# One block of values and sums per unit, and two heads' softmax sums by PE, in an attention and expert kernel

## The reference

```python
xn = layernorm(x)
q = (xn @ Wq.T).reshape(b, t, 8, 32)
kv = xn @ Wkv_down.T                     # rank 64
k = (kv @ Wk_up.T).reshape(b, t, 8, 32)
v = (kv @ Wv_up.T).reshape(b, t, 8, 32)
attn = softmax(einsum('bqhd,bkhd->bhqk', q, k) * 32 ** -0.5)
a = einsum('bhqk,bkhd->bqhd', attn, v).reshape(b, t, 256) @ Wo.T
e = mod(floor(xn @ wr + br), 8)          # the expert of each token
y = relu(xn @ W1[e] + b1[e]) @ W2[e] + b2[e]
out = x + a + y
```

## Time and profile before

| what | before |
|---|---|
| median of 3 runs | 508.03 us (506.31 to 508.95) |
| the profiled execution | 507.6 us |
| its span, first to last instruction | 505.8 us |
| mean granted clock of TensorE | 0.97 |
| busy: PE / DVE / Pool / ACT | 90% / 83% / 77% / 69% |
| first stage, units 2 to 15 | about 86 to 231 us of the span |
| second stage, units 16 to 31 | about 344 to 504 us of the span |

### The profile page before, as it was taken

How to read it: one execution, slowest core, us unless ns; L and a number is a source line. 1 busy time by engine, 2 the same in 40 slices (tenths; PEclk the granted TensorE clock), 3 DMA queues, 4 the chain that set the end, 5 groups by cost and what they waited for, 6 DMA issues and landing times.

```text
span 505.8 us, 15098 instructions
## 1 busy us (share of the span) xinstructions
PE 453.2 (90%) x4992; PEld 318.6 (63%) x4992; DVE 418.0 (83%) x885; ACT 347.1 (69%) x864; POOL 388.0 (77%) x407
## 2 busy tenths in 40 slices
PE   1577886999899898998999999998999999999997
PEld 1356443656566464656999999994657656666565
DVE  6998964768998999977888788886698898988986
ACT  3777463767777677766777777774577667876775
POOL 5546287888888988883777777776788888989883
PEclk9985797999999999999999999999899999999999
DMA  8794233444757678589687888845356565765522
GB/s 233 227 181 128 63 79 84 107 96 95 204 123 186 164 224 235 153 260 252 211 264 245 271 262 280 257 152 116 83 124 134 142 128 118 149 134 128 111 80 89
DMA packets 81930, 83.07 MB, mean 164 GB/s; under 512 B 10608, under 2 KB 66384, under 8 KB 81872
## 3 DMA queue, kind: packets, MB, share of 16 engines
q1 hardware_dynamic: 77520, 73.40, 54.5%
q0 software_dynamic: 4352, 8.92, 7.7%
HBM read 38.61 MB, written 18.37 MB: 113 GB/s over the span
## 4 chain that ended last, share of the span: by engine, by line
PE 43%; POOL 24%; DVE 9%; issue 9%; DMA 8%; ACT 4%; SPq 3%; ACTq 0%; POOLq 0%; DVEq 0%
POOL xsort L602 11%; POOL padd L633 11%; PE psum L1286 5%; PE psum L1409 5%; PE psum L1270 4%; PE psum L1251 4%; DMA stk<-mT 4%; PE psum L1392 3%; PE psum L1410 3%; PE psum L1393 3%; PE psum L1394 3%; DVE negm L992 3%; PE psum L1328 3%; SPq L328 2%; PE psum L1301 2%
## 5 line engine op out<-in xcount | busy, mean ns | idle before, releaser
L719 ACT ACTIVATE prob<-psum 128x512 f32<-128x512 f32 x256 | 150.1, 593 | 101.7 <-PE psum L1270 100.9
L992 DVE TENSOR_REDUCE negm<-psum 128x2 f16<-128x512 f32 x256 | 170.3, 681 | 42.1 <-PE psum L1251 41.2
L633 POOL TENSOR_TENSOR padd<-prob 128x512 f32<-128x512 f32 x104 | 125.7, 1209 | 27.7 <-ACT prob L719 21.3
L1251 PE MATMUL psum<-stk 96*128 96x256 f16 x512 | 101.2, 280 | 12.9 <-DVE negm L992 11.6
L584 POOL TENSOR_TENSOR padd<-xTl,padd 128x512 f16<-128x512 f32 x71 | 82.3, 1159 | 32.6 <-DVE padd L1104 32.6
L1270 PE MATMUL psum<-stk 97*128 97x256 f16 x512 | 97.5, 274 | 5.9 <-DMA stk<-mT 3.8
L789 ACT ACTIVATE xTl<-psum,xn_all 128x128 f32<-128x128 f32 x284 | 81.1, 369 | 26.7 <-POOL padd L584 18.1
L602 POOL DMA_INDIRECT xsort<-xn_all,pos x64 | 71.7, 1121 | 15.7 <-issue 13.7
L1251 PEld LDWEIGHTS psum<-stk 96*128 96x128 f16 x512 | 42.2, 98 | 54.1 <-DVE negm L992 28.3
L610 POOL DMA_INDIRECT xn_all<-ysort,pos x64 | 66.0, 1031 | 11.1 <-issue 7.9
L1286 PE MATMUL psum<-prob,vt 128*32 128x256 f32 x1024 | 70.2, 393 | 0.0
(11 more groups left out here) (171 smaller groups left out, 890.9 us busy)
## 6 DMA issues: line engine op xcount, KB each, us to landing
stk<-split SPq DMA_DIRECT2D x192, 128.0 KB
xn_all<-wsplit SPq DMA_DIRECT2D x71, 258.0 KB, 4.7
xTh<-xsort SPq DMA_DIRECT2D x18, 256.0 KB, 4.2
ysort<-xTh SPq DMA_DIRECT2D x18, 256.0 KB, 4.6
out<-acc SPq DMA_DIRECT2D x15, 256.0 KB
acc<-x SPq DMA_DIRECT2D x3, 1024.0 KB, 8.4
xn_all<-W SPq DMA_DIRECT2D x12, 256.0 KB
wsplit<-xn_all SPq DMA_DIRECT2D x12, 256.0 KB, 3.3
```

The costliest lines, as they stand in the source:

```text
L633: nc.gpsimd.tensor_tensor(padd[:, bb, hs], prob[:, bb, hs, 0, :], prob[:, bb, hs, 1, :], ALU.add).then_inc(pool_add, 1)
L719: nc.scalar.activation(prob[:, bb, h, :, :].rearrange("p a c -> p (a c)"), bank[st_bank(u, n)], ACT.Exp, scale=SCALE).then_inc(act_exp, 1)
L992: V.tensor_reduce(negm[:, k % 2, col:col + 2], bank[n % 2].rearrange("p (a c) -> p a c", a=2), AX.X, ALU.max, negate=True).then_inc(dve_ma ...
L1251: ins = mm(bank[n % 2][:, qc * T:(qc + 1) * T], stk[0:96, s, 1, h, t0 + qc * P:t0 + (qc + 1) * P], stk[0:96, s, 0, h, t0:t0 + T], start=Tr ...
```

## The change

Three edits. Pool no longer adds the key chunks behind pair 3 (heads 2 and 3 of the first batch); it adds behind pairs 1 and 5, and in the second stage also 6. PE instead sums these two heads from the two chunks, with four matmuls that accumulate in place of two. And the two places of values and sums on PE become one: both batches' blocks stand at n = 4, behind the scores of pair 4 and the v projection, the second batch of unit u-1 first and the first batch of unit u behind it. In the last two units the sums are those of before, at the new place.

```diff
@@ Pool
-                    if u < NU - 2 and n in (1, 3, 5, 6)[:3 + u // (NU // 2)]:
+                    if u < NU - 2 and n in ((1, 5, 6) if u >= NU // 2 else (1, 5)):
@@ sums
-                    pe.wait_ge(pool_add, u * 4 - NU // 2 + 2 * bb + 2 if half else u * 3 + bb + 2)
+                    pe.wait_ge(pool_add, u * 3 - NU // 2 + 2 * bb + 1 if half else u * 2 + bb + 1)
                     if bb == 1:
                         pe.wait_ge(dve_add, u + 1)
-                for h in range(HG):
+                whole = 2 if bb == 0 and not late else HG
+                for h in range(whole):
                     ins = mm(bank[4 + bb][h * HD:(h + 1) * HD, T:2 * T], ones[:, 0:HD], padd[:, bb, h, :],
                              start=True, stop=True)
+                for kc in range(2):
+                    for h in range(whole, HG):
+                        ins = mm(bank[4 + bb][h * HD:(h + 1) * HD, T:2 * T], ones[:, 0:HD], prob[:, bb, h, kc, :],
+                                 start=(kc == 0), stop=(kc == 1))
                 ins.then_inc(pe_pv, 1)
@@ body of PE
-                        if n == 2 and not f:
-                            values(u * 2 - 1, k + 3, 1, it * 2 + (k + 1) // 2 * 2)
-                            sums(u - 1, 1, last and k == 3, half)
...
-                        if n == 7:
+                        if n == 4:
+                            if not f:
+                                values(u * 2 - 1, k + 3, 1, it * 2 + (k + 1) // 2 * 2)
+                                sums(u - 1, 1, last and k == 3, half)
                             values(u * 2, k, 0, sbu * 2 + 1, u + 2 if nxt else u + 1)
                             sums(u, 0, last and k >= 2, half)
```

## The result

The kernel after takes 571.98 us (median of 4 runs, 569.67 to 574.16) against 508.49 for the kernel before beside it (506.31 to 510.52): a ratio of 1.126, 95% interval 1.120 to 1.131. It is 63.5 us slower; the forecast was 54 us slower, 562, with a range of 545 to 578. The profiled execution took 574.16, the longest of the four, with a span of 572.3 and a mean granted clock of 0.961.

A forecast was written before the change was run, and what follows sets the result against it. Pool was taken to bound the first stage and PE the second. Terms of 26.1 - 2.0 + 4 + 20.0 + 2.4 + 3.6 gave +54 us on 508, so 562, with 0.8 lying within 545 to 578.

The forecast's parts named there:

- PE's leg and the block's length: PE from transpose to scores 5: 1.15 us plus a merged block of 3.30, making 4.45.
- Two legs in series: Each unit: PE's leg of 4.45 us, then DVE's of 5.97 in the second stage, one waiting for the other.
- Odd unit 12.73: Second stage, odd units: output projection behind pair 5 and residual add 1.89 us to 10.84, giving 12.73.
- First stage: Units 4 to 13, before the experts: 127.2 us against 107.2, so +20.0.
- Even unit 11.2: Second stage, even units: 11.0 us with the q projection's wait, 11.2 with the expert sum slowed beside a Pool addition.
- Units 17 to 30: Second stage, transpose 17 to transpose 30: 129.3 us becomes 156.3 less 0.9 for missing projections, +26.1.
- The end: From the last transpose on: exp of pair 4 waits for later sums, output projection uncovered; +4 us (0 to +5).
- Rival 3, the clock: PE's idle waits lower its clock and a quarter of its legs double, +32 us: 594; chance 0.10.
- Up to unit 4: Start to unit 4's transpose: Pool's 1.25 us and a slow block gained, units 2 and 3 lose 3.7; +2.4.
- Pool's relief is swallowed: Less Pool work, worth at most 1.2 us a unit, gains nothing: new legs exceed Pool's old period of 10.98.
- Rival 1: Legs overlap and Pool's relief shows, DVE idling under about 0.5 us a unit behind the block: 503; chance 0.06.
- Rival 2: Transpose's wait or v copy costs less than laid out, about 1 us a unit less over 29 units: 533; chance 0.10.

The follow-up runs named there:

- e1: Kernel before with only Pool's pair 3 addition dropped and PE summing heads 2 and 3, both blocks at their old places: 506.78 us, ratio 0.998.
- e6: Kernel after, but heads 2 and 3 of the first batch take the sums of heads 0 and 1, two matmuls instead of four: 565.49 us, ratio 1.103.
- e3: Kernel after with the second batch's block back behind pair 2, the first batch's staying behind pair 4: 534.37 us, ratio 1.050.
- e4: Kernel after with the first batch's block back behind pair 7, the second batch's staying behind pair 4: 554.32 us, ratio 1.091.
- e7: Kernel after with DVE's addition of the experts' results moved from n = 6 to n = 4: 576.88 us, ratio 1.126.
- e9: Kernel after, but from unit 17 Pool's second-batch additions take only 16 of 256 columns of each head: 573.91 us, ratio 1.120.
- e12: Kernel before, unchanged, run again on a third chip for another trace: 512.58 us.
- e10: Kernel before with only Pool's pair 3 addition given to PE, blocks unmoved, a repeat on another chip: 524.69 us, ratio 1.021.

## Why the prediction was right, and where it was off

The terms, between the same transposes in the two traces:

| stretch | forecast | measured |
|---|---|---|
| up to the transpose of unit 4 | +2.4 | +5.5 (106.69 to 112.15) |
| units 4 to 14 | +20.0 | +20.4 (107.2 to 127.6) |
| unit 14 to 16, through the experts | +3.6 | +4.9 |
| unit 16 to 17 | -2.0 | -2.3 (12.63 to 10.29) |
| units 17 to 30 | +26.1 | +31.0 (129.3 to 160.2) |
| the end | +4 | +7.2 (16.4 to 23.6) |
| sum | +54 | +66.5 |

- *PE's leg and the block's length*: right to 0.05 us. The unknown in it, one round for the four accumulating matmuls, is 0.43 (e1) and 0.40 to 0.44 (e6, by the periods).
- *Two legs in series*: right. DVE's idle time ahead of row maximum 5, the transpose's wait of 0.9 for the normalisation and the q projection's wait of 0.49 to 0.85 for the values' copy all stand in the trace of after, and e6 shows that a round more or less of PE work moves the unit by its own length, beside 1.5 us of idle time on PE. e3 and e4 show that both moves matter, the block taken from n = 2 more.
- *Odd unit 12.73*: 12.7 to 12.84.
- *First stage* (127.2 for ten units): 127.6, but this agreement is partly luck. The odd units with a weight split took 13.5, not 13.95; the even units 6 and 8 took 11.86 and 11.72, not 11.25; and unit 12 took 13.70, of which some 1.6 is PE at the lower level of its clock (unit 10, with the same work, took 12.07). The first stage of e7 and e9 is the same program and took 129.5 and 129.0.
- *Even unit 11.2*: 11.64, the one term of a unit of the second stage that was too small. The place of the two operations was right: Pool's addition starts 5.75 behind the transpose and the expert sum 6.39 (forecast 5.7 and 6.4). The price was not. I had the row for it (an expert sum of 1.82 beside an addition) and took only 0.2, where the sum alone grew by 0.50; and the key addition, which now lies beside Pool's pair 6 addition, I had taken at its short length. Together they add 0.86 to DVE's leg, of which e9 shows 0.55 on the path: with both short the even unit is 11.07 to 11.18, near the 11.0 that I had before adding for the fight.
- *Units 17 to 30* were 4.9 too long. The even units miss 2.2 in all (five of the six 0.43 to 0.51 each); the odd ones 0.3 in all; unit 29, partly at the lower level of the clock (14.18), 1.5; and the 0.9 that I took off for missing projections didn't show.
- *The end*: the transpose of the last unit waited 1.79 us for the normalisation, and the block behind it ran at the lower level of the clock:

```profile
548.70 0.27 PE L1314 MATMUL psum<-ident,negm 128*128 128x128 f16 x1 [1.79 <-DVE oT L999]
...
550.61 1.94 PE L1286 MATMUL psum<-prob,vt 128*32 128x256 f32 x16
```

The windows of after there and at unit 29 (stretch and its length, busy us of PE, its weight load, DVE, ACT and Pool, granted clock, DMA share, GB/s):

```profile
531.00:534.00 3.00, 1.61 (x12) 0.94 (x12) 3.00 (x6) 1.87 (x5) 2.80 (x4) 1.00 0.09 22
534.00:537.00 3.00, 2.69 (x17) 1.57 (x19) 1.67 (x4) 0.91 (x3) 2.54 (x3) 0.51 0.16 36
...
549.00:552.00 3.00, 3.00 (x24) 1.57 (x26) 0.22 (x1) 0.27 (x1) 1.65 (x2) 0.50 0.44 133
552.00:555.00 3.00, 3.00 (x40) 1.35 (x32) 0.55 (x2) 1.29 (x3) 0.00 (x0) 0.58 0.11 22
```

- *Rival 3, the clock*, came true in part. Of the blocks of attention units in after, the values took 1.94 at 87.74 (unit 2), 1.94 at 214.40 (unit 12), 1.93 at 241.44 (unit 14) and 1.94 at 550.61 (unit 30), and in unit 29 the block was partly slow (1.34 at 536.85); the blocks between have 1.07. In units 12 and 14 the wait ahead of the transpose was the 0.91 of the other units, PE had been busy 1.55 of the 3 us before, and the granted clock then read 0.53 and 0.58; at 534, PE had been busy 1.61 of 3. From unit 12:

```profile
212.58 0.23 PE L1314 MATMUL psum<-ident,negm 128*128 128x128 f16 x1 [0.91 <-DVE oT L999]
...
214.40 1.94 PE L1286 MATMUL psum<-prob,vt 128*32 128x256 f32 x16
```

Units 2, 12, 14 and 29 are longer than like units (4, 10, 4 and 27) by 2.3, 1.6, 1.6 and 1.4, about 7 us in all by this estimate, more than half of the 12.4 by which the span overran the forecast. I had given the clock a chance and no term. The Trainium skill (TensorE: Matmul & The Clock Gate, Why this matters for your kernels) warns of idle gaps between bursts; the trace agrees only in part, since waits of 0.9 stood ahead of blocks of 1.07 in most units and of 1.93 and 1.94 in two. A term for the ends of the stages could have been drawn from the rows, since there a wait of 1.91 has values of 1.93 behind it; the falls in units 12 and 14 could not, and in e7 and e9, with the same program there, they are absent.
- *Up to unit 4*: 3.1 more than forecast. 1.24 of it stands already at the transpose of unit 0 (60.03 against 58.79), ahead of any block that was moved. The slow block of before (83.54) that I had counted as gained did not go: after has one of the same length at 87.74, now in unit 2, which took 13.65. How much is spread can't be told: e12, the kernel before again, is 1.5 later than its first trace at unit 0 and 3.7 later at unit 4.
- *Pool's relief is swallowed*: right. Pool waits 120.1 us for exponentials in after. That Pool paced the first stage of before is less sure than I wrote: e12 has shorter periods there and reaches the last of them no earlier.
- *Rival 1* (503) needed less than 0.5 us of idle time on DVE a unit; there are 3.1. *Rival 2* (533), less waiting than laid out, didn't come: both waits have about their full length.

## What to carry to other kernels

When two engines hand work to each other through a few buffers, the work that one of them does without feeding the other must come in portions no longer than the buffers cover; here merging two portions was to save 0.2 us of switching a unit; it put 3.1 us of idle time on the other engine in one piece and lengthened the unit by 2.2 to 2.4. Add up the legs of both engines between two hand-overs before moving a block, and count who shares the bank in the new place. Where two engines slow each other, price it by how far their operations overlap in the new order, and measure an edit worth under 2% on more than one chip, since the same kernel can settle into another pattern.

## What the hardware showed that I had not expected

- Where a DVE operation with two inputs in SBUF starts during a Pool addition, it grows by the time they overlap, less some 0.13: the expert sum takes 0.68 alone, 1.01 with 0.46 us of the addition beside it (e10), 1.17 to 1.22 with 0.61 to 0.68 (after, e1), 1.71 with 1.16 (e10) and 1.82 with 1.27 (before). That addition keeps its 1.27 to 1.29. Where the DVE operation started first, it was Pool's that grew: in the odd units of after the sum keeps 0.68 with 0.22 of the pair 6 addition beside it, and that addition takes 0.80 to 0.82 instead of 0.73. So the order of starting decides which of the two pays.
- One unchanged kernel gave ratios of 0.998 and 1.021 to a kernel before run beside it, on two chips; both medians rest on runs that agree within 1.3% among themselves.
- A low spell of the clock need not come back with the same program: after has one in each of units 12 and 14 (values 1.94 and 1.93), e7 and e9, with the same first stage, have none there. And slow matmuls are not always the clock: in e7 the values took 1.38 instead of 1.05 at a granted clock of 1.00.
